# Self-attention from bf16 part stacks through DRAM to fp32 operands held in SBUF

## What is computed

```python
# layer 0 self-attention: 16 heads of 16, q, k, v each normed per head, no mask
q = _layernorm((x @ Wq + bq).reshape(b, s, 16, 16), q_scale, q_bias)   # k, v alike
probs = softmax(einsum('bqhd,bkhd->bhqk', q, k) * 16 ** -0.5)
x = x + einsum('bhqk,bkhd->bqhd', probs, v).reshape(b, s, 256) @ Wo + bo
# layer 1 self-attention: the same without the norms per head, causal
logits = where(triu(ones((s, s)), 1), -inf, einsum('bqhd,bkhd->bhqk', q, k)) / 4
```

## Time and profile before

| | |
|---|---|
| median of three runs | 2077.92 us |
| the profiled execution (span) | 2074.9 us |
| PE busy | 1461.4 us, 8446 matmul records |
| DVE busy | 1322.2 us |
| ACT busy | 835.9 us |
| POOL busy | 371.6 us |
| DMA moved | 116.29 MB |

### The profile page before, as it was taken

One profiled execution on the slowest core, in us unless ns is written; L12 is line 12 of the kernel. 1 busy time (PEld: TensorE's weight loads), 2 busy tenths in 40 slices (PEclk: granted clock), 3 DMA queues, 4 the chain that ended last, 5 costly groups with the idle time before them and its releaser, 6 DMA issues. The chain is left out here.

```text
span 2074.9 us, 30519 instructions
## 1 busy us (share of the span) xinstructions
PE 1461.4 (70%) x8446; PEld 757.8 (37%) x8447; DVE 1322.2 (64%) x5100; ACT 835.9 (40%) x1658; POOL 371.6 (18%) x274
## 2 busy tenths in 40 slices
PE   4769998998983344434365366988998884369994
PEld 2432222222233333323243232434435673136662
DVE  6989787887528999999841466776753457601112
ACT  2732666666763322222231240655565553111110
POOL 2760000000003222223302351000000332210003
PEclk9966999999997777777677695999999997679997
DMA  7184232221000000000014258224400022651003
GB/s 245 61 200 64 35 43 43 32 40 17 24 1 1 1 1 1 1 1 1 1 44 137 64 159 161 42 42 67 58 2 1 9 39 36 218 175 31 30 20 91
DMA packets 122611, 116.29 MB, mean 56 GB/s; under 512 B 47010, under 2 KB 95966, under 8 KB 122468
## 3 DMA queue, kind: packets, MB, share of 16 engines
q1 hardware_dynamic: 116087, 103.12, 22.5%
q0 software_dynamic: 3072, 8.39, 1.3%
q10 hardware_dynamic: 3312, 3.02, 0.4%
HBM read 72.74 MB, written 41.49 MB: 55 GB/s over the span
## 5 line engine op out<-in xcount | busy, mean ns | idle before, releaser
L1016 DVE TENSOR_REDUCE arena<-banks 128x1 f32<-128x512 f32 (+1 forms) x896 | 514.5, 627 | 163.1 <-PE banks L872 86.8
L976 ACT ACTIVATE arena<-banks 128x512 f32<-128x512 f32 (+3 forms) x896 | 430.1, 557 | 325.1 <-PE banks L889 180.6
L872 PE MATMUL banks<-arena 96*128 96x512 bf16 (+1 forms) x896 | 334.4, 397 | 39.8 <-DMA arena<-v 20.2
L889 PE MATMUL banks<-arena 98*128 98x512 bf16 (+3 forms) x896 | 291.1, 367 | 11.0 <-ACT arena L976 5.1
L1209 PE MATMUL banks<-arena 128*77 128x128 f32 x512 | 86.2, 324 | 213.8 <-POOL arena L1332 207.6
L1322 POOL TENSOR_TENSOR arena<-arena 128x1232 f32<-128x1232 f32 x48 | 108.7, 2265 | 693.4 <-DVE arena L1382 434.1
L906 PE MATMUL banks<-arena 128*32 128x512 f32 (+3 forms) x1792 | 219.0, 564 | 16.7 <-ACT arena L976 12.8
L1370 DVE MATCH_REPLACE8 arena<-arena 128x77 f32<-128x77 f32 x1024 | 213.7, 224 | 0.0
L872 PEld LDWEIGHTS banks<-arena 96*128 96x128 bf16 x896 | 86.3, 100 | 268.3 <-DVE arena L1016 174.2
L1864 DVE COPY arena<-banks 128x1024 f32<-128x1024 f32 x23 | 28.2, 1224 | 205.0 <-PE banks L1803 205.0
L1209 PEld LDWEIGHTS banks<-arena 128*77 128x77 f32 x512 | 74.4, 181 | 225.1 <-POOL arena L1332 211.1
(11 more groups left out here) (214 smaller groups left out, 2019.1 us busy)
## 6 DMA issues: line engine op xcount, KB each, us to landing
arena<-parts SPq DMA_DIRECT2D x192, 128.0 KB, 7.1
arena<-in_L_ffn_W SPq DMA_DIRECT2D x16, 1024.0 KB, 12.0
parts<-arena SPq DMA_DIRECT2D x24, 512.0 KB, 8.4
v<-arena SPq DMA_DIRECT2D x32, 256.0 KB, 2.3
arena<-v SPq DMA_DIRECT2D x16, 512.0 KB, 10.5
arena<-sorted SPq DMA_DIRECT2D x46, 128.0 KB, 2.1
sorted<-arena SPq DMA_DIRECT2D x10, 512.0 KB, 9.2
expert_out<-arena ACTq DMA_DIRECT2D x23, 128.0 KB, 2.4
```

The costliest lines, as they stand in the source:

```text
L872: mm = pe.matmul(PS[:, f % NBK, 0:w], qst[r][0:KS, j, i * P:(i + 1) * P], kst[r][0:KS, j, kb * BANK:kb * BANK + w], start=True, stop=not diag)
L889: mm = pe.matmul(bank, kst[r][0:KM, j, kt * P:(kt + 1) * P], qst[r][0:KM, j, c0:c1], start=True, stop=not diag)
L976: act.activation(prob[(kt * G + j) % PR][:, c0:c1], PS[:, NBK + n % NBK, 0:c1 - c0], ACT.Exp, scale=SCALE).then_inc(sem(s + "_exp"), 1 if ...
L1016: dve.tensor_reduce(m2[:, j, i, kb:kb + 1], PS[:, f % NBK, 0:w], AX.X, ALU.max).then_inc(sem(s + "_red"), 1)
```

## The change

The bf16 parts, their split and the DRAM buffers go (`split_chunks`, `store_parts`, `load_unit`, `store_projections`, `stack_buffers`). Queries and keys of both batches stay in SBUF as fp32, four heads to a tile of 128 partitions, head j in rows 32j to 32j+15; row 32j+16 of the keys is 1 and that of the queries takes the negative maximum. Values lie in SBUF as well.

```diff
+        KT_AT = work_mark
+        QT_AT = KT_AT + NU * S
+        V_AT = QT_AT + NU * S // 2
```

Both passes take 16 or 17 rows at row 32j. A first-pass entry is two heads into two neighbouring banks; there are two such pairs of banks (0, 1 and 2, 3), and DVE takes both heads' maxima in one instruction. Transposed maxima and outputs go through the same ring of pairs. The second pass uses banks 4 to 6, the weighted values bank 7, for one half (512) of the queries at a time:

```diff
+                def scores(n, u, f):
+                    i, kb, pair, w = unit_fills[f]
+                    diag = causal and kb == i * P // BANK
+                    for j in (2 * pair, 2 * pair + 1):
+                        row = slice(SLOT * j, SLOT * j + HD)
+                        bank = PS[:, 2 * (n % 2) + j % 2, :]
+                        mm = pe.matmul(bank[:, 0:w], queries(u)[row, i * P:(i + 1) * P], keys[row, u, kb * BANK:kb * BANK + w],
+                                       start=True, stop=not diag)
+                        if diag:
+                            mm = pe.matmul(bank[:, w - P:w], identb, future, start=False, stop=True)
+                    mm.then_inc(sem(s + "_fill"), 1)
...
+                def second_pass(u, gi, j):
+                    half, kt, lo = groups[gi]
+                    n = (u * NGR + gi) * G + j
+                    row = slice(SLOT * j, SLOT * j + KM)
...
+                    mm = pe.matmul(bank, keys[row, u, kt * P:(kt + 1) * P], queries(u)[row, half * BANK + lo:(half + 1) * BANK],
                                    start=True, stop=not diag)
                     if diag:
                         mm = pe.matmul(bank[:, 0:P], identb, futureT, start=False, stop=True)
...
+                        dve.tensor_reduce(m2[u % 2][:, 2 * pair:2 * pair + 2, i, kb], PS[:, 2 * (n % 2):2 * (n % 2) + 2, 0:w],
+                                          AX.X, ALU.max).then_inc(sem(s + "_red"), 1)
```

The order on PE is a list made beforehand (`ring`), spread over the steps by columns. The loops are written out. A unit goes like this, and waits are as shown:

```diff
+                        if n >= 2:
+                            pe.wait_ge(sem(s + "_red"), n - 1)
...
+                    if n >= 3:
+                        pe.wait_ge(sem(s + "_exp"), n - 2)
...
+                for u in range(NU):
+                    pe.wait_ge(sem(s + "_rows"), 16 * G * (u + 1))
+                    for gi in range(NGR):
                         for j in range(G):
+                            first_pass(upto[u][gi * G + j])
+                            second_pass(u, gi, j)
+                            if j == 1 and gi:
+                                weighted(u, gi - 1)
+                            elif j == 1 and u:
+                                weighted(u - 1, NGR - 1)
```

```diff
+                            for k in range(KD):
+                                pe.matmul(dst, hT[:, k, i * P:(i + 1) * P], w_qkv0[:, k, n0:n0 + nw], start=(k == 0), stop=False)
+                            mm = pe.matmul(dst, first_row, w_qkv0[:, 2, n0:n0 + nw], start=False, stop=True)
...
+            chunks = [(b, g, qk, half) for b in range(B) for g in range(NG) for qk in range(2) for half in range(S // BANK)]
...
+                        mm = pe.matmul(PS[:, i % 4, :], w_qk1[:, k, (qk * NG + g) * P:(qk * NG + g + 1) * P],
                                        hT[:, k, b * S + half * BANK:b * S + (half + 1) * BANK],
                                        start=(k == 0), stop=(k == KD - 1))
```

More of the change, by code:

```diff
@@ L75, in fills, with key_groups @@
         for k in range(0, keys, BANK):
-            out.append((i, k // BANK, min(BANK, keys - k)))
+            for pair in range(G // 2):
+                out.append((i, k // BANK, pair, min(BANK, keys - k)))
+    return out
+def key_groups(causal):
+    out = []
+    for half in range(S // BANK):
+        for kt in range(TB):
+            lo = max(0, kt * P - half * BANK) if causal else 0
+            if lo < BANK:
+                out.append((half, kt, lo))
     return out
@@ L579, in qkv0 @@
         def qkv0(block):
             s = "q0"
[L581 removed]
+            (first, own), keys, values = heads_of()
+            R.at = SMALL_AT
             ss = [R.f32(3 * NH) for _ in range(4)]
[L583 to L588 removed]
@@ L729, in dest @@
-            def dest(i, n):
-                b, m, half = where(i)
-                return parts[b][:, n, m, half * BANK:(half + 1) * BANK]
-            act_split, second_rest, third_rest = split_chunks(s, u_bufs, source, dest)
+            (first, own), keys, values = heads_of()
+            chunks = [(b, g, qk, half) for b in range(B) for g in range(NG) for qk in range(2) for half in range(S // BANK)]
+            NCH = len(chunks)
+            def dest(i):
+                b, g, qk, half = chunks[i]
+                unit = keys[:, b * NG + g] if qk else (first, own)[b][:, g]
+                return unit[:, half * BANK:(half + 1) * BANK]
@@ L956, in _, with weighted @@
-                with pe.Fori(0, 2) as i:
-                    for r in range(NST):
-                        unit((i, r))
-                unit((2, 0), units_left=1)
-                unit((2, 1), units_left=0)
-                turn_output((2, 1))
+                def weighted(u, gi):
+                    half, kt, lo = groups[gi]
+                    pe.wait_ge(sem(s + "_exp"), (u * NGR + gi + 1) * G)
+                    if kt == 0 and (u or half):
+                        pe.wait_ge(sem(s + "_o"), 2 * u + half)
+                    for j in range(G):
+                        mm = pe.matmul(PS[SLOT * j:SLOT * (j + 1), 7, lo:BANK], values[:, u // NG * TB + kt, u % NG * G + j, :],
+                                       prob[:, gi % 2 * G + j, lo:BANK], start=(kt == 0), stop=(gi == last_of[half]))
+                    mm.then_inc(sem(s + "_pv"), 1)
```

1016 lines of the change are left out of this document (438 added, 578 removed).

## The result

The changed kernel takes 3509.93 us (median of four runs, 3505.45 to 3513.83) against 2078.43 us of the kernel before (four runs, 2072.51 to 2083.48): 1.689 times as long, interval 1.686 to 1.693. Forecast were 2485 us and a range of 2280 to 2740. Slower was right; the size was not, and the number is the one of rival C.

A forecast was written before the change was run, and what follows sets the result against it. PE was taken to bound the attentions. From 2074.9: -19 projections and +114 attention of layer 0, +5 projections and +308 attention of layer 1 give 2483, plus 3 for the median of runs: 2485 us, range 2280 to 2740.

The forecast's parts named there:

- rival C: Both attentions: PE's granted clock falls to its lower level, 1.2 of 2.4 GHz; 124 and 155 us a unit, about 3500; 2%.
- three steps: Attention, layer 0: between two weighted groups PE needs three steps of 0.858 us; a key group costs 3.75 us.
- rival B: Both attentions: row groups don't overlap; 131 us a unit in layer 0, 95 in layer 1, total 3087; 6%.
- the lower bound (two steps): Attention, layer 0: all four row groups always full, two steps between groups, no hand-overs; 48 us a unit, -39.
- estimate by the 3.07x: Attention, layer 0: packing figure for four 32-row tiles; a step 1.12 instead of 0.86 us, stage another 87 us longer, sum 2572.
- Mask matmuls over all 128 rows separate the heads: Attention, layer 1: each diagonal mask needs all row groups, so heads can't overlap there; 34.3 us of scores a unit one after another.
- a unit of layer 1: Attention, layer 1: scores, masks, changes of shape, weighted values and transposes together 80 us a unit, of 41 before; stage +308.
- Projections of layer 1: Padded slots double the query and key columns: 70 us against 64.8, +5 (0 to +15).
- Rival A: Both attentions: row groups fill the array, masks hold nobody back, DVE sets the pace; 41 and 31 us a unit, total 1905; 10%.
- The prologue: Attention, layer 0: 40 first entries at 1.15 to 1.22 us and the landing of the maxima, 50 us (51 before).
- The last unit: Attention, layer 0: the unit without first pass, at ACT's pace as before, 40 us.
- Projections of layer 0: PE becomes the bound at 4.9 us a tile; attention starts at 121 instead of 140, -19 (bounds -25 and 0).

## Why the prediction was wrong, point by point

**The failed step: the clock.** The sum has every duration at the level that the earlier trace rows happened to show, and rival C, with the measured result (3500; units of 124 and 155 us, measured 123.3 and 145.5), got 2% on the ground that PE would wait less than now. PE did wait less: it was busy 96% of the stage in layer 0 (91% before) and 99.6% in layer 1. The clock was 0.52 and 0.51 all the same, and rows in use decided it: 16 or 17 of each 32 give 0.52 and 32 give 0.87 with the same list of instructions in layer 0; 96 rows give 0.93 and 32 to 34 give 0.51 in the kernel before. The step took busy time for work done by the array. Rival C had the number without the cause: it drew the low level from short matmuls that wait, and PE hardly waited. The hint stood in the earlier trace rows: the slices at 0.6 were read as ones in which PE had waited, and I didn't ask what else a matmul of 16 rows lacks.

The Trainium skill, "TensorE: Matmul & The Clock Gate", section "What's actually happening", says that the throttle is released by activity, by how busy PE has been recently. Read as busy share, the trace disagrees: 1151.87 of 1157 us busy at 0.51, and the measurement decides; read as work in the array, the runs fit it. They don't settle what exactly is counted: rows were varied, at 16, 32, 34, 96 and 128, but columns and the share of time at each were not. The number of rows isn't all of it: in the kernel before, matmuls of 96 rows ran at 0.50 from 142 to 180 us, where 61 of them took 36.48 us. And the stretch of 30.7 us at the full clock amid the changed layer 0 has no cause that I can show.

**What was right.** Row groups overlap, and three steps are the price of a key group where nothing waits: 3.86 us for 3.75 at the full clock. In the kernel with 32 rows seven of the sixteen groups of a unit take 4.71 us, in part for a wait of 0.66 us for ACT's exponentials; the unit is 70.2 us, and the sum had 70 with 8 of hand-overs. So at the full clock the unit of layer 0 was forecast right, and rival B and the lower bound (two steps) were wrong. The prediction's estimate by the 3.07x of the Trainium skill, "TensorE: Matmul & The Clock Gate", Part 3, has a step of 1.12 us, which would make the shortest key group 4.5 us and a unit 82; the traces have 3.86 and 70.2 and disagree. Mask matmuls over all 128 rows separate the heads: leaving them out took 559 us away. A mask with its changes of shape costs 0.35 us at the full clock, where the sum had 0.335, and a unit of layer 1, at the lower clock, 145.5 us for 80: 1.8 times as much. Projections of layer 1 took 69.0 us for 70. DVE is busy 36%, and one maximum for two heads brought no gain that could be measured. Rival A needed a unit under 52 us in layer 0: even with 32 rows the stage is 685 us. The Trainium skill, "TensorEngine Tiling (Array Packing)", Theoretical Speedup, has up to four times for contractions of 32 or less. Here four heads do start together, and a whole unit of layer 0 gains 1.85 times at the full clock (129.9 us one after another, 70.2 with 32 rows side by side), but the weighted values and the waits don't shrink with it, and no kernel of these came near A's 1905 us.

**The two ends of layer 0** were both put too low. The prologue was put at 50 us and is 97 until the second pass begins (168.8 to 266.1 us): the first scores no longer hide under DVE's 46 us at the lower clock. It is part of the same mistake, and the one part that 32 rows don't mend (97 us at 0.52). The last unit was put at 40 us, at ACT's pace. With 32 rows it takes about 65 us even where its clock is 0.95, with 3.86 us from one weighted group to the next and PE waiting 0.67 us for ACT in each: the two engines wait for each other in turn, which the sum had left out.

**Projections of layer 0: wrong in sign.** -19 forecast, +28.8 measured. A tile takes 7.49 us (PE's transposes start at 103.20 and 110.69) instead of 4.9. The waits of that stage (who for whom, total us, times, longest), PE's timeline and ACT's say why:

```profile
PE banks L544 <- ACT arena L569: 35.3, 15, 2.6
```

```profile
103.20 1.06 PE L544 MATMUL banks<-arena 128*128 128x128 f32 x8 [2.55 <-ACT arena L569]
...
110.69 1.06 PE L544 MATMUL banks<-arena 128*128 128x128 f32 x8 [2.55 <-ACT arena L569]
```

```profile
100.69 0.81 ACT L557 ACTIVATE arena<-banks 128x768 f32<-128x768 f32 x1 [5.12 <-PE banks L531]
...
101.62 0.77 ACT L566 ACTIVATE arena<-banks,arena 128x512 f32<-128x512 f32 x1
102.28 0.77 ACT L569 ACTIVATE arena<-banks,arena 128x512 f32<-128x512 f32 x1
```

The transposes go into banks that ACT has only just copied out (L566, L569), and these copies stand behind a later tile's squares in ACT's order, which wait for PE's projections (L531). So PE and ACT take turns: PE's 4.9 us of work, as forecast, and then 2.55 us of waiting for ACT, together the 7.49. The sum priced every engine by its work and took the highest; the wait that the moved bias and scale added was never named. No experiment changed this, so the 48 us against the forecast have their place from the trace alone.

**The range** was built of bounds within one mechanism; the clock, a factor of two on two stages forecast at 1218 us together, was left to a rival of 2%.

## What to carry to other kernels

Before a plan makes matmuls smaller, ask for the granted clock after it, not only for the time that they fill: here a unit of layer 0 took 129.9 us with its matmuls one after another at full height, 70.2 with four groups of 32 rows side by side, and 123.3 with 16 or 17 rows of each group in use, which gave nearly all of the gain back. Fill the 32 rows (padding them took no time here) and compare with the plain full-height form. A full-height instruction strewn between row groups takes the overlap away from both sides, so move such work (a mask) to another engine or behind several heads. A mask isn't needed at all where only an upper bound of the maximum is wanted, as long as the masked scores don't lie so far above the others that all exponentials vanish.

Price an engine's work and its waits apart: where two engines hand a bank to and fro, as in the projections here, their times add up.

## What the runs showed of the hardware that was not expected

- PE busy 99.6% of 1157 us at a granted clock of 0.51; full-height matmuls in the same places 1.00.
- Four fp32 heads overlapped with 16 rows at the lower level: 1033 us; one after another with 128 rows at the full: 1057 us. The second kernel is the faster one in total, 3027 to 3510.
- The kernel before with a third of its rows takes 625 us longer.
- Adding rows that are nearly all zeros to every matmul raises the clock (0.52 to 0.87 in layer 0) and shortens the program by 403 us.
- In the changed layer 0 30.7 us run at the full clock amid the lower one, with the same instructions before and behind; the two units that share them took 113.5 and 110.3 instead of 123.3 us. In another run with the same instructions the stretch stood elsewhere.
- The last unit of layer 0 ran at 0.95, 0.66 or 0.50 in kernels whose layer 0 is the same.
